# Count matrices of strips 0 to 4 from visits of four targets with 196 keys

## The reference

```python
h = jnp.maximum(_layernorm(x, axis=-1), 0.0)
x = x + _L0_gnn_ref(h, edge_index, W1, b1, W2, b2)              # two graph convolutions
h = jnp.maximum(_layernorm(x, axis=-1), 0.0)
x = x + _L1_gnn_ref(h, edge_index, edge_attr_32, W1, b1, W2, b2)  # messages with attributes, mean by target
...
def gcn_conv(x, edge_index, W, b):
    h = x @ W
    ...                                                          # loops added, dinv from the degrees
    msg = h[src] * norm[:, None]
    return jax.ops.segment_sum(msg, dst, num_segments=n) + b
```

## Time and profile before

| | |
|---|---|
| median of 3 runs | 3141.37 us |
| lowest, highest | 3138.80, 3148.31 us |
| profiled execution, its own time | 3138.66 us |
| its span (first to last instruction) | 3136.9 us |
| mean granted TensorE clock | 0.929 |
| first aggregation (first unit to last strip's add) | 318.97 to about 1230 us |
| second aggregation | about 1294 to 1700 us |
| message stage and update | from about 1771 us |

### The profile page before, as it was taken

The page is one execution under the profiler, slowest core; times in us unless marked ns, Lnnn a source line. Parts: engine busy times, 40 slices in busy tenths (PEclk is TensorE's granted clock), DMA queues, the critical chain, the costliest instruction groups (busy, mean ns, idle before and its releaser), DMA issues.

```text
span 3136.9 us, 52738 instructions
## 1 busy us (share of the span) xinstructions
PE 2606.1 (83%) x17613; PEld 2020.3 (64%) x17614; DVE 1754.2 (56%) x4923; ACT 930.9 (30%) x2523; POOL 1782.9 (57%) x1739
## 2 busy tenths in 40 slices
PE   2655678899999897799997588989898888999887
PEld 0124356677777887688886466766666666666666
DVE  7889998888766775400001744444444444444446
ACT  6413023445566674300000222222222222222220
POOL 2860562344444552256652177777777777777772
PEclk9995999999999998889998799899999999898999
DMA  7112111222232442456553222222222222222222
GB/s 309 34 39 82 29 45 46 96 97 97 91 147 99 162 163 107 157 171 232 225 224 132 85 77 77 77 69 70 74 76 76 76 77 77 77 76 77 76 77 60
DMA packets 120006, 324.33 MB, mean 103 GB/s; under 512 B 42594, under 2 KB 79303, under 8 KB 113335
## 3 DMA queue, kind: packets, MB, share of 16 engines
q0 software_dynamic: 57616, 96.07, 12.0%
q10 hardware_dynamic: 6624, 147.72, 11.6%
q1 hardware_dynamic: 55593, 78.37, 7.4%
HBM read 200.50 MB, written 121.53 MB: 103 GB/s over the span
## 4 chain that ended last, share of the span: by engine, by line
PE 37%; POOL 28%; DVE 17%; issue 12%; DMA 2%; ACT 2%; DVEq 1%; POOLq 0%; SPq 0%; ACTq 0%
POOL rows L595 26%; PE ps_feat L860 12%; PE ps_node L860 12%; DVE region_c L1624 6%; PE ps_pre L846 3%; DVE region_c L1619 2%; PE ps_turn L846 2%; PE ps_extra L846 1%; POOL region_b L642 1%; DMA rows<-table,idx 1%; POOL visit_start L647 1%; DVE rows L1468 1%; ACT rows L1057 1%; PE ps_pre L849 1%; PE ps_sum L968 1%
## 5 line engine op out<-in xcount | busy, mean ns | idle before, releaser
L595 POOL DMA_INDIRECT rows<-table,idx x1088 | 1044.7, 960 | 608.2 <-issue 326.4
L617 POOL DMA_INDIRECT permuted<-edge_rows_of,slot_of_edge x544 | 597.0, 1097 | 585.4 <-ACT region_a L1126 442.9
L1624 DVE TENSOR_SCALAR region_c<-iota_key,region_c 128x392 bf16<-128x392 f16 (+1 forms) x2328 | 544.7, 309 | 0.0
L860 PE MATMUL ps_node<-region_a,region_b 128*128 128x256 bf16 x3528 | 454.3, 274 | 1.8 <-ACT region_b L1088 1.8
L860 PE MATMUL ps_feat<-region_a,region_b 128*128 128x256 bf16 x3528 | 453.6, 276 | 0.0
L1606 DVE TENSOR_TENSOR rows<-rows,ps_pre 128x512 f32<-128x512 f32 x256 | 175.6, 686 | 482.5 <-DMA rows<-table,idx 308.2
L1178 ACT ACTIVATE rows<-rows 128x512 f32<-128x512 f32 x256 | 161.3, 630 | 805.6 <-DVE rows L1606 805.6
L860 PEld LDWEIGHTS ps_feat<-region_a,region_b 128*128 128x128 bf16 x3528 | 348.6, 99 | 56.8 <-issue 3.7
L860 PEld LDWEIGHTS ps_node<-region_a,region_b 128*128 128x128 bf16 x3528 | 346.4, 99 | 58.6 <-ACT region_b L1088 2.0
L961 PE MATMUL ps_pre<-edge_w,region_a 128*128 128x512 f32 x512 | 298.4, 668 | 62.5 <-DMA region_a<-attr_t_in 62.5
L968 PE MATMUL ps_sum<-onehot,rows 128*128 128x64 f32 x2048 | 287.6, 287 | 24.4 <-ACT rows L1178 24.3
(11 more groups left out here) (252 smaller groups left out, 3454.8 us busy)
## 6 DMA issues: line engine op xcount, KB each, us to landing
counts<-region_a ACTq DMA_DIRECT2D x24, 3136.0 KB, 9.7
region_a<-counts ACTq DMA_DIRECT2D x22, 3136.0 KB
rows<-table,idx POOLq DMA_INDIRECT x1088, 2.6
region_a<-attr_t_in SPq DMA_DIRECT2D x64, 256.0 KB, 2.7
permuted<-region_b SPq DMA_DIRECT2D x17, 833.0 KB, 23.3
region_a<-permuted SPq DMA_DIRECT2D x17, 833.0 KB, 4.9
edge_rows_of<-edge_cols_in POOLq DMA_DIRECT2D x16, 578.0 KB
permuted<-edge_rows_of,slot_of_edge POOLq DMA_INDIRECT x544
```

The source lines that it names most:

```text
L595: nc.gpsimd.indirect_dma_start(rows[:, s, j * D:(j + 1) * D], None, tables[n], bass.IndirectOffsetOnAxis(ap=idx[:, h, k:k + 1], axis=0),). ...
L617: nc.gpsimd.indirect_dma_start(permuted, bass.IndirectOffsetOnAxis(ap=slot_of_edge[:, r * RT + k:r * RT + k + 1], axis=0), edge_rows_of[:, ...
L860: ins = mm(strip_bank(buf), parts[:, h, k], counts[buf][:, h], start=(h == 0 and k == 0), stop=(h == SB - 1 and k == PARTS - 1), skip_grou ...
L1624: ins = v.tensor_scalar(hot_key[:, u % 2, j, 0:n], iota_key[:, 0:n], visit_keys[:, at:at + 1], None, ALU.is_equal)
```

## The change

In strips 0 to 4 every window gets two groups of visits, one for each four of its targets, with 196 keys, as the windows of strips 16 to 23 have. `SPLITS[w]` holds the numbers of visits of the two groups (or of the one whole group in strips 5 to 15, which keep their plan). `build_window` sums each group into its own half of the bank. The visits' plan (`visit_of`) gives every group its own first target and starts its visits at that target's first edge. The numbers of visits by strip become 404, 201, 189, 128 and 128 in place of 373, 176, 144, 128 and 128.

```diff
--- before.py
+++ after.py
@@ -48,8 +48,10 @@
 ROW = 16
 
 
-FIRST_VISITS = (59, 26, 20, 17, 15, 14, 13, 12, 11, 11, 10, 10, 10, 9, 9, 9, 9, 8, 8, 8, 8, 8, 7, 7, 7, 7, 7, 7, 7, 7, 7, 6)
-RUNS = (((2, 6), (2, 5)), ((2, 5), (2, 4)), ((4, 4),), ((4, 4),)) + 5 * (((4, 3),),) + 14 * (((4, 2),),)
+FIRST_HALVES = (42, 18, 14, 12, 11, 10, 9, 9, 8, 8, 8, 7, 7, 7, 7, 6, 6, 6, 6, 6, 6, 6, 6, 5, 5, 5, 5, 5, 5, 5, 5, 5,
+                5, 5, 5, 5, 5, 5, 4, 4, 4, 4, 4, 4, 4, 4, 4, 4, 4, 4, 4, 4, 4, 4, 4, 4, 4, 4, 4, 4, 4, 4, 4, 4)
+HALF_RUNS = ((9, 4), (116, 3), (131, 2))
+WHOLE_RUNS = ((5 * SW, 3), (6 * SW, 2))
 TURN_AFTER = {(2, 0): 0}
 TURN_AFTER_APPLIED = {4: 0}
 CW = 64
@@ -72,8 +74,11 @@
 KEYS = W * SB
 
 
-HALVED_FROM = 16 * SW
-VISITS = list(FIRST_VISITS) + [k for runs in RUNS for n, k in runs for _ in range(n * SEG)]
+half_visits = list(FIRST_HALVES) + [k for n, k in HALF_RUNS for _ in range(n)]
+SPLITS = [tuple(half_visits[k:k + 2]) for k in range(0, len(half_visits), 2)] + [(k,) for n, k in WHOLE_RUNS for _ in range(n)]
+SPLITS += (NW - len(SPLITS)) * [(1, 1)]
+VISITS = [sum(k) for k in SPLITS]
+KEYS_OF_VISIT = [KEYS // len(SPLITS[w]) for w in range(NW) for _ in range(VISITS[w])]
 VB = (sum(VISITS) + P - 1) // P
 EDGE_ROWS = EP // ROW + max(VISITS) * (P // ROW)
 PARTS = 3
@@ -86,7 +91,7 @@
 assert DT % (SLOTS * TC) == 0 and TURNS - FIRST_TURN == 2 * RANGES and sum(UNIT_TILES) == SB and RT % 2 == 0
 assert DT * P >= RANGE_ROWS
 assert all((b - a) * SB <= 512 for a, b in TILE_GROUPS) and RT * P < OWN_EDGE and RANGES % RANK_BATCH == 0 and DU == 2 * SLOTS - 2
-assert sum(PACED) == RANGES and P % UNIT == 0 and VISITS[HALVED_FROM:] == [2] * (NW - HALVED_FROM)
+assert sum(PACED) == RANGES and P % UNIT == 0
 
 
 def build(nc, t, out):
@@ -408,12 +413,6 @@
 
         def visits_upto(w):
             return sum(VISITS[:w])
-
-        HALVED_VISITS = visits_upto(HALVED_FROM)
-
-        def keys_of(at):
-
-            return KEYS // 2 if at >= HALVED_VISITS else KEYS
 
         MARKED = sorted({visits_upto(w + 1) for w in range(NW)} | set(range(UNIT, sum(VISITS) + 1, UNIT)))
 
@@ -837,18 +836,16 @@
 
                 bank = count_banks[w % BANKS][:, 0:KEYS]
                 pe.wait_ge(C["evacuated"], w + 1)
-                first, end = visits_upto(w), visits_upto(w + 1)
-                for at in range(first, end):
+                at = visits_upto(w)
+                n = KEYS // len(SPLITS[w])
+                for part, k in [(part, k) for part, visits in enumerate(SPLITS[w]) for k in range(visits)]:
                     u, j = at // UNIT, at % UNIT
                     if j == 0:
                         pe.wait_ge(C["hot"], u + 1)
-                    if w < HALVED_FROM:
-                        ins = mm(bank, hot_src[:, u % 2, :, j], hot_key[:, u % 2, j], start=(at == first),
-                                 stop=(at == end - 1), skip_group_check=True)
-                    else:
-                        ins = mm(bank[:, (at - first) * (KEYS // 2):(at - first + 1) * (KEYS // 2)], hot_src[:, u % 2, :, j],
-                                 hot_key[:, u % 2, j, 0:KEYS // 2], start=True, stop=True, skip_group_check=True)
-                    if at + 1 in MARKED:
+                    ins = mm(bank[:, part * n:part * n + n], hot_src[:, u % 2, :, j], hot_key[:, u % 2, j, 0:n], start=(k == 0),
+                             stop=(k == SPLITS[w][part] - 1), skip_group_check=True)
+                    at += 1
+                    if at in MARKED:
                         ins.then_inc(C["built"], 1)
 
             def strip_bank(buf):
@@ -1620,7 +1617,7 @@
                                     visit_lo[:, None, u * UNIT:(u + 1) * UNIT].to_broadcast([P, P, UNIT]), ALU.is_equal)
                     for j in range(UNIT):
                         at = u * UNIT + j
-                        n = keys_of(at)
+                        n = KEYS_OF_VISIT[at] if at < len(KEYS_OF_VISIT) else KEYS
                         ins = v.tensor_scalar(hot_key[:, u % 2, j, 0:n], iota_key[:, 0:n], visit_keys[:, at:at + 1], None, ALU.is_equal)
                     ins.then_inc(C["hot"], 1)
 
@@ -1869,9 +1866,10 @@
     at = ROW * np.arange(EDGE_ROWS)[:, None] + np.arange(P)[None, :]
 
     visit_of = np.zeros((3, VB * P), np.int32)
-    target_of = np.concatenate([w * W + (np.zeros(k, int) if w < HALVED_FROM else np.arange(2) * (W // 2)) for w, k in enumerate(VISITS)])
+    parts_of = [(w * W + j * (W // len(SPLITS[w])), k) for w in range(NW) for j, k in enumerate(SPLITS[w])]
+    target_of = np.concatenate([np.full(k, target) for target, k in parts_of])
     visit_of[0, :sum(VISITS)] = target_of
-    visit_of[1, :sum(VISITS)] = np.concatenate([np.arange(k) * (w < HALVED_FROM) for w, k in enumerate(VISITS)]) * (P // ROW)
+    visit_of[1, :sum(VISITS)] = np.concatenate([np.arange(k) for _, k in parts_of]) * (P // ROW)
     visit_of[2, :sum(VISITS)] = -target_of * SB
     visit_of = visit_of.reshape(3, VB, P).transpose(2, 0, 1)
     node_half = P * np.arange(SB)[None, :] + np.arange(P)[:, None] - 0.5
```

## The result

The changed kernel takes 3069.59 us (median of 4 runs, 3067.41 to 3070.74) against 3143.66 us for the kernel before in the same comparison: a ratio of 0.9764, 95% interval 0.9749 to 0.9780. A second comparison gave 3076.24 against 3143.40, 0.9786 (0.9770 to 0.9802). 3063 was forecast. The profiled execution took 3068.60 us for a span of 3066.8.

The account below looks back on a forecast made before the run. No engine bounds the whole; VectorE bounds strips 0 to 4, VectorE and TensorE strips 5 to 9, TensorE the later ones. 38.0 + 9.0 + 10.1 + 5.0 + 13.8 = 75.9 us off 3138.7 gives 3063 us, range 3050 to 3090.

Parts of the forecast that it names:

- What a unit costs: VectorE's unit of eight visits in strips 0 to 4 falls from 2.46 to 2.05 us with 196 keys.
- Term one: Strips 0 to 4: 132 units of 2.05 us replace 119 of 2.46; 292.6 us, 38.0 us less.
- 3 us of waits and 1 us for the start: Part of Term one: what remains in strips 0 to 4 of 17.1 us of slow start and waits.
- the 2.15 from which the prediction would have called itself wrong: Sign of failure: half units in strips 0 to 4 farther apart than 2.15 us in the mean.
- Term three: Strips 5 to 23: TensorE's clock falls after waits at strip ends vanish, 13.8 us less.
- Term two: Later strips start with 6 visits made, not 3: 9.0 us less in strips 10-15, 10.1 in 16-23, 5.0 in 5-9.
- the reserve that the range named: Strips 5 to 9 might win some 5 us more, as other products fall into each unit.
- near 2.4 us: In Term three, the idle time of TensorE after which its clock falls; with 1.0 to 1.3 us none expected.
- The rival from the Trainium skill: TensorE at half clock through strips 1 to 4: 67 us more, 3130 us; strip 0 hides it; chance 0.03.
- The fallback: Any half window with more edges than its visits read makes `full` redo both aggregations: over 6500 us; chance 0.02.
- nothing took the place of the late unit: Rival: at strip ends something else finishes as late, so the shift gives nothing; only Term one left, 3101 us; chance 0.05.
- waits of the old size did not stay: Rival: the 17 us of waits in strips 0 to 4 stay, 3076 us; chance 0.08.

Follow-up runs that it names:

- the late add: VectorE adds a strip only after the next strip's first unit: on the changed kernel 0.9716 and 0.9648 (3032.41 us), on the kernel before 0.9761 (3069.03 us).
- experiments 1 and 2: 1: kernel before, five more whole visits in the first window, 0.9894 and 0.9908; 2: changed kernel, three more half visits ending strip 4, 0.9892 and 0.9899.
- experiment 4: Changed kernel with the late add and half visits from strip 12 on in place of strip 16: 3013.61 us, ratio 0.9588.

## Why the prediction was right, and where it was off

The two mechanisms held, the cheaper unit and the later strips' shift against the units, and the strips gave 68.1 us of the 75.9 forecast. That 3063 lies as near to 3069.59 as it does is in part luck: the node phase between the aggregations, which is not in the sum, was 5.5 us shorter in this profile (see below), and what follows it 3.2 us longer.

- **What a unit costs** held: 2.05 us with half keys, in strip 0 too, and 132 units.
- **Term one** gave 30.4 in place of 38.0 us. Of the 300.16 us, 132 units take 270.6, the turn 12.12 - 2.05 = 10.1 (10.0 forecast), and the ends of strips 8.7 (8.0). The rest is 10.8, where "3 us of waits and 1 us for the start" was taken. The start cost nothing. The ordinary waits, 0.12 us at every second or third unit, add up to 3.3, as priced. The other 7.5 are single late units, each behind products that TensorE does at half speed or near it (six in 1.21 to 1.49 us, 0.82 at full clock): 1.6 at the start of strip 1, 0.8 early in strip 2, 2.2 after the edge turn, 1.6 and 1.3 after the ends of strips 2 and 3. With them half units stand (300.16 - 10.1 - 8.7) / 132 = 2.13 us apart in the mean, just under the 2.15 from which the prediction would have called itself wrong. Term three looked for falls of the clock in strips 5 to 23 only; the step that failed is that the waits in strips 1 to 4 were priced at full clock. The last two are of a kind: in the six profiles without the late add eight of the twelve ends of strips 2 and 3 bring a late unit, in the three with it none of six, so there they come from the wait.
- **Term two** held. The experiments 1 and 2 separate it from the half visits in both directions. It was 1.37 us of idle time for 1.5 in strips 10 to 15. Strips 5 to 9 gave 6.6 beyond the clock where 5.0 were taken: with three visits to a window, other products fall into each unit, the reserve that the range named. The 4.6 us that stay between the two kernels with the late add point the same way.
- **Term three** held: with waits of 1.04 to 1.48 us no strip from 5 on shows a clock below 1.00. But "near 2.4 us" was too high a mark for where it starts: a fall followed the 2.03 us before 547.52, though not the 2.03 us before 547.37 in the second profile. At the ends of strips 2 and 3 such a fall comes in some executions and not in others, and the sum had nothing for it.
- **The rival from the Trainium skill** (TensorE: Matmul & The Clock Gate, the section on a second failure mode) came true in strip 0, where the granted clock is 0.50 to 0.53 for more than 100 us after the change. In that section the Trainium skill tells of a swing between the two levels. This profile shows the lower one nearly throughout strip 0; a granted clock between the two, 0.63 to 0.67 in parts of strip 0, is seen only in others. As a lasting half clock it did not come in strips 1 to 4, where the granted clock is 0.92 to 0.95. Its price in strip 0 was nothing, as that rival had it.
- The fallback did not occur, nothing took the place of the late unit, and waits of the old size did not stay.

Not in the sum was the node phase between the aggregations, the same code in all kernels. It took 81.9 us before and 76.4 after:

```profile
1230.00:1311.60 81.60, 48.25 (x309) 41.11 (x310) 44.96 (x103) 34.93 (x65) 5.71 (x6) 0.75 0.27 90
```

```profile
1162.00:1238.30 76.30, 43.12 (x310) 36.81 (x311) 44.68 (x103) 34.94 (x65) 4.84 (x6) 0.87 0.29 96
```

It is shorter where the granted clock comes back earlier, 0.87 against 0.75. Over the other profiles with fast transfers it is 74.7 us at 0.91 (the changed kernel with the late add), 76.4 at 0.89 (the kernel before with it), 79.5 at 0.81 (the changed kernel again) and 81.6 at 0.75 (experiment 4), so it is not the change's. It was left open what decides it.

## What to carry to other kernels

Where an in-order engine feeds another in batches, look at what it does at the end of each stage before it makes the next batch. A wait for the consumer placed ahead of the production empties the pipe each time, and how many items the last batch happens to hold beyond the end then decides how long. Here more than half of the gain of a change of the data's layout was that accident. Putting the wait one batch later takes all of it and more, 60 us against 38 in strips 5 to 23 of the kernel before, without any change of the layout. Before a gain is put down to an edit, count what it does to the rounding of batches.

## What the runs showed of the hardware

- A wait of 2.03 us was followed by a fall of TensorE's clock from its upper level (2.4 GHz) to its lower one (1.2 GHz) in one profile of the changed kernel; in the other the same wait at the same place was not. The changed kernel's waits of 1.04 to 1.48 us in strips 5 to 23 never were, and the 2.27 us before 1048.91 in the kernel before were not either. The length of the wait alone does not decide.
- With eight half visits of 0.09 us in each 2.05 us TensorE was at its lower level nearly all through strip 0 in the profile of the changed kernel (0.50 to 0.53), and for part of the time in others (0.66). With sixteen it stayed at the upper one (0.98 and 0.99).
- VectorE's key one-hot costs 231 ns from start to start at 392 columns and 180 at 196. By a straight line through the two, an estimate, 129 ns of it don't depend on the columns.
- The same kernel took 3143 us on one chip and 3775 and 3770 on two others. Strips 5 to 15 of experiment 1's kernel on those two agreed to 0.1 us with the changed kernel's on the first; the difference lay in other stretches, the second aggregation and what follows it above all.
